# A graph-attention edge phase re-blocked: node groups at every 484th edge, four chunks to a block, TensorE work in 64-row halves

## What is computed

```python
h = (x @ W.T).reshape(n, H, D)                  # 6250 x 8 heads x 32
alpha = einsum('ehd,hd->eh', h[src], a_src) + einsum('ehd,hd->eh', h[dst], a_dst)
enc = relu(edge_attr @ edge_W.T + edge_b).reshape(-1, H, D)
alpha = leaky_relu(alpha + sum(enc * h[dst], -1), 0.2)
ex = exp(alpha - segment_max(alpha, dst)[dst])
attn = ex / maximum(segment_sum(ex, dst)[dst], 1e-10)
out = segment_sum(h[src] * attn[..., None], dst)  # sum over the edges that end in a node
```

## Time and profile before

| | |
|---|---|
| median of 3 runs | 8268.06 us (8252.19 to 8271.06) |
| the profiled execution | 8254.24 us, its span 8252.5 us |
| PE / DVE / ACT / POOL busy over the span | 75% / 56% / 35% / 52% |
| DMA engines' mean share | 31.0% of 16 engines for DMAs issued by SP, 25.4% for POOL's |
| mean granted TensorE clock | 0.923 of 2.4 GHz |

### The profile page before, as it was taken

One profiled execution on the slowest core, in us unless ns is written; L12 is line 12 of the kernel. 1 busy time (PEld: TensorE's weight loads), 2 busy tenths in 40 slices (PEclk: granted clock), 3 DMA queues, 4 the chain that ended last, 5 costly groups with the idle time before them and its releaser, 6 DMA issues. The chain is left out here.

```text
span 8252.5 us, 163611 instructions
## 1 busy us (share of the span) xinstructions
PE 6179.6 (75%) x32278; PEld 4927.6 (60%) x32278; DVE 4611.0 (56%) x15207; ACT 2868.2 (35%) x5703; POOL 4286.7 (52%) x4324
## 2 busy tenths in 40 slices
PE   0279999999999999319999176666666666663793
PEld 0166666666666666319998165555555555552792
DVE  2337777777777777611111447777777777764005
ACT  0025555555555555102222023333333333331120
POOL 0027777777777777140000437777777777771103
PEclk9989999999999999659999589999999999995896
DMA  1446666666666666625555436666666666674453
GB/s 48 144 106 155 153 153 153 153 154 155 153 153 153 153 153 154 188 87 174 186 180 184 135 91 160 159 160 160 158 157 161 159 160 159 159 147 140 162 187 129
DMA packets 1526846, 1244.98 MB, mean 151 GB/s; under 512 B 1112600, under 2 KB 1256875, under 8 KB 1500779
## 3 DMA queue, kind: packets, MB, share of 16 engines
q1 hardware_dynamic: 1316073, 648.43, 31.0%
q0 software_dynamic: 205472, 580.68, 25.4%
q10 hardware_dynamic: 5256, 15.41, 0.6%
HBM read 1106.73 MB, written 137.14 MB: 151 GB/s over the span
## 5 line engine op out<-in xcount | busy, mean ns | idle before, releaser
L732 POOL DMA_INDIRECT e_rows<-sc_table,e_idx x3900 | 3878.0, 994 | 1409.0 <-issue 1084.7
L791 PE MATMUL e_ps_o<-e_rows,e_pt 128*128 128x256 f32 x7840 | 1892.1, 389 | 475.1 <-ACT e_pt L848 455.9
L791 PEld LDWEIGHTS e_ps_o<-e_rows,e_pt 128*128 128x128 f32 x7840 | 1454.5, 194 | 735.4 <-issue 562.7
L776 PE MATMUL e_ps_s<-e_ident,e_arep 128*128 128x128 f32 x7840 | 1048.1, 282 | 344.9 <-ACT e_arep L842 341.7
L776 PEld LDWEIGHTS e_ps_s<-e_ident,e_arep 128*128 128x128 f32 x7840 | 962.1, 195 | 465.8 <-issue 460.5
L836 ACT ACTIVATE e_encr<-e_ps_e 128x640 f32<-128x640 f32 x786 | 553.5, 704 | 1353.4 <-PE e_ps_e L763 1340.0
L984 DVE CUSTOM_DVE_ANT_0 e_x<-e_ps_s,e_mask 128x640 f32<-128x640 f32 x784 | 645.1, 823 | 641.4 <-PE e_ps_s L776 631.5
L772 PE MATMUL e_ps_s<-e_encr,e_bd 128*128 128x512 f32 (+1 forms) x3136 | 956.0, 448 | 0.8 <-ACT e_encr L836 0.8
L842 ACT COPY e_arep<-e_rows 128x640 f32<-128x640 f32 x786 | 570.7, 726 | 993.9 <-DMA e_rows<-sc_table,e_idx 993.5
L1514 POOL DMA_INDIRECT c_g<-sc_yb,f_slot_i x147 | 170.9, 1162 | 1346.5 <-PEq L1496 1288.3
L772 PEld LDWEIGHTS e_ps_s<-e_encr,e_bd 128*128 128x128 f32 x3136 | 504.0, 191 | 481.9 <-issue 481.9
(11 more groups left out here) (271 smaller groups left out, 6126.7 us busy)
## 6 DMA issues: line engine op xcount, KB each, us to landing
e_dstb<-sc_dstp SPq DMA_DIRECT2D x792, 320.0 KB
x_w<-in_L_ffn_W_dram SPq DMA_DIRECT2D x112, 1024.0 KB
e_rows<-sc_table,e_idx POOLq DMA_INDIRECT x3960
x_w<-in_L_ffn_w_dram SPq DMA_DIRECT2D x60, 1024.0 KB
sc_xb<-r_zero SPq DMA_DIRECT2D x24, 1024.0 KB
x_xin<-sc_xb SPq DMA_DIRECT2D x86, 256.0 KB
sc_yb<-x_y SPq DMA_DIRECT2D x82, 256.0 KB
e_at<-sc_attrp SPq DMA_DIRECT2D x396, 45.0 KB
```

The costliest lines, as they stand in the source:

```text
L732: pool.indirect_dma_start(rows[0:CK, k, j, :], None, dr["table"][:, :], bass.IndirectOffsetOnAxis(idx[0:CK, k, j:j + 1], 0)).then_inc(s_ro ...
L776: mm = nc.tensor.matmul(banked(ps_s)[:, j, :], arep[0:CK, p, j, :, :].rearrange("p t h -> p (t h)"), ident[0:CK, 0:CK], start=not first, s ...
L791: mm = nc.tensor.matmul(ps_o[:, p, 0:D], pt[0:CK, p, j * P:(j + 1) * P], rows[0:CK, k, j, 0:D], start=(j == 0), stop=(j == CH - 1))
```

## The change

- **Windows.** A group of nodes begins at the node of every 484th edge (STEP), 427 groups; a group with more than 16 nodes is cut into windows of 16. A window still has 16 rows of nodes, but it begins at any node, and only the nodes up to the group's end count. A later group's store overwrites rows that an earlier one wrote beyond its end.
- **Blocks** have four chunks: BE = 512.
- **Row order** is head-major: partition = head x 16 + node, before node x 8 + head. `wc` and `agg` are addressed with three levels (8 heads, 16 nodes, words).
- **Score.** `bd` is 64 columns to a half; half 0 goes to PSUM rows 0 to 63, half 1 to 64 to 127, in turns by 256 edges. **Aggregation** multiplies 64 weight columns (4 heads) by the 128 columns of these heads, for each of two groups.
- **PSUM tiles** `ps_e`, `ps_s`, `ps_t` have two banks, used in turns; the encoder's 512 columns are one matmul.
- **Attributes.** `attrp` has 12 rows, and the load of a block reads them three times with a stride of zero.
- **Plan.** Group starts and ends are read with strided DMAs; the search goes over 806 pieces of 256 words and issues 14 gathers of 256 words, up to four in flight; ACT and POOL split the attributes.

```diff
-MEAN = -(-E * WIN // N)
-CH = -(-(MEAN + 2 * int(MEAN ** 0.5)) // P)
+STEP = 484
+NI = -(-E // STEP)
+MAXW = NI + -(-N // WIN)
+RB = 256
+NR = P * EC // RB
+CH = 4
...
             for s in range(2):
+                pool.wait_ge(s_rix, s + 1)
                 for t in range(WT):
                     k = s * WT + t
-                    if k:
-                        pool.wait_ge(s_cp, k)
-                    pool.indirect_dma_start(rows[:, 0, :], None, (dr["pmax"] if s == 0 else dr["smin"])[:, :],
-                                            bass.IndirectOffsetOnAxis(rix[:, s, t:t + 1], 0)).then_inc(s_wg, 16)
-                    pool.wait_ge(s_wg, 16 * (k + 1))
+                    if k >= 4:
+                        pool.wait_ge(s_cp, k - 3)
+                    pool.indirect_dma_start(found[:, k % 4, :], None,
+                                            (dr["pmax"] if s == 0 else dr["smin"]).rearrange("(r k) -> r k", k=RB),
+                                            bass.IndirectOffsetOnAxis(rix[:, s, t:t + 1], 0)).then_inc(s_wg[k % 4], 16)
...
-                sp.dma_start(wc[:, k, :], dr["wcol"].rearrange("(w t) (h c) -> w (t h) c", t=WIN, c=2)[bass.ds(w, 1), :, :]
-                             .rearrange("a p c -> (a p) c")).then_inc(s_load[k], 16)
+                sp.dma_start(wc[:, k, :], dr["wcol"][bass.ds(n, WIN), :].rearrange("t (h c) -> h t c", c=2)).then_inc(s_load[k], 16)
...
-                    sp.dma_start(at[:, k, :], dr["attrp"][:, bass.ds(e, BE)]).then_inc(s_load[k], 16)
+                    sp.dma_start(at[:, k, :], dr["attrp"][:, bass.ds(e, BE)].unsqueeze(0).to_broadcast([3, PARTS, BE])).then_inc(s_load[k], 16)
...
-                sp.dma_start(dr["agg"].rearrange("(w t) (h c) -> w (t h) c", t=WIN, c=DH)[bass.ds(w, 1), :, :]
-                             .rearrange("a p c -> (a p) c"), res[:, k, :]).then_inc(s_out, 16)
+                sp.dma_start(dr["agg"][bass.ds(n, WIN), :].rearrange("t (h c) -> h t c", c=DH), res[:, k, :]).then_inc(s_out, 16)
...
                 lhs = w_enc[:, half * P:(half + 1) * P]
-                nc.tensor.matmul(banked(ps_e)[:, 0:4, :], lhs, cols[:, 0:4, :], start=True, stop=True)
-                nc.tensor.matmul(banked(ps_e)[:, 4, :], lhs, cols[:, 4, :], start=True, stop=True).then_inc(s_enc, 1)
+                nc.tensor.matmul(ps_e[:, half, :], lhs, at[:, k, :], start=True, stop=True).then_inc(s_enc, 1)
...
-                    for half in range(2):
-                        hold(pe, s_relu, b * 2 + (half + 2), s_pp)
-                        for c0, c1 in ((0, 4), (4, CH)):
-                            nc.tensor.matmul(banked(ps_s)[:, c0:c1, :], bd[:, p, half, :], chunks(encr[:, p, half, :])[:, c0:c1, :],
-                                             start=(half == 0), stop=False, skip_group_check=True)
+                    hold(pe, s_relu, b * 2 + 3, s_pp)
+                    for c in range(0, BE, BE // 2):
+                        for half in range(2):
+                            nc.tensor.matmul(ps_s[half * (P // 2):(half + 1) * (P // 2), p, c:c + BE // 2], bd[:, p, half, :],
+                                             encr[:, p, half, c:c + BE // 2], start=(c == 0), stop=False, skip_group_check=True)
...
                 for j in range(CH):
-                    mm = nc.tensor.matmul(ps_o[:, p, 0:D], pt[0:CK, p, j * P:(j + 1) * P], rows[0:CK, k, j, 0:D],
-                                          start=(j == 0), stop=(j == CH - 1))
+                    for g in range(GROUPS):
+                        mm = nc.tensor.matmul(ps_o[g * GP:(g + 1) * GP, p, 0:GH * DH], pt[:, p, j * P + g * GP:j * P + (g + 1) * GP],
+                                              rows[:, k, j, g * GH * DH:(g + 1) * GH * DH], start=(j == 0), stop=(j == CH - 1))
```

More of the change, by code:

```diff
@@ L110, in plan_phase @@
         pt = ps("pt", [P, 512])
-        pb = ps("pb", [P, 512])
+        pb = ps("pb", [P, 1024])
         pc = ps("pc", [P, 512])
+        pn = ps("pn", [P, 2, 1024])
         s_in, s_attr, s_pad, s_const, s_pe, s_tab = (sem(n) for n in ("in", "attr", "pad", "const", "pe", "tab"))
-        s_out, s_row, s_wq, s_wg, s_bt = (sem(n) for n in ("out", "row", "wq", "wg", "bt"))
-        s_pass, s_split = sem("pass"), sem("split")
+        s_out, s_row, s_wq, s_bt, s_rix, s_zp = (sem(n) for n in ("out", "row", "wq", "bt", "rix", "zp"))
+        s_pass, s_split, s_rest, s_bl, s_grid = (sem(n) for n in ("pass", "split", "rest", "bl", "grid"))
         s_win, s_go, s_cp, s_step, s_chain, s_tile = (sem(n) for n in ("win", "go", "cp", "step", "chain", "tile"))
-        s_ends, s_scan, s_final, s_parts, s_nb, s_cum, s_blk = (sem(n) for n in ("ends", "scan", "final", "parts", "nb", "cum", "blk"))
+        s_ends, s_scan, s_final, s_iv, s_cumi, s_nb, s_cum, s_blk = (
+            sem(n) for n in ("ends", "scan", "final", "iv", "cumi", "nb", "cum", "blk"))
+        s_wg = [sem(f"wg{k}") for k in range(4)]
+        full = NI // P
         block = ctx.enter_context(nc.Block())
@@ L157, in _ @@
         def _(sp):
[L158 to L162, removed]
+            sp.wait_ge(s_pad, 1)
+            v = io["dst"]
+            sp.dma_start(dst_i[0:P - 1, :], v[0:(P - 1) * EC].rearrange("(p e) -> p e", p=P - 1)).then_inc(s_in, 16)
+            sp.dma_start(dst_i[P - 1:P, 0:E_LAST], v[(P - 1) * EC:E].rearrange("(p e) -> p e", p=1)).then_inc(s_in, 16)
+            sp.wait_ge(s_pad, 3)
             v = io["edge_attr_3"]
@@ L165, in _ @@
             sp.dma_start(attr[P - 1:P, 0:E_LAST, :], v[(P - 1) * EC:E, :].rearrange("(p e) c -> p e c", p=1)).then_inc(s_attr, 16)
-            sp.wait_ge(s_in, 64)
-            sp.wait_ge(s_pad, 6)
+            v = io["src"]
+            sp.dma_start(src_i[0:P - 1, :], v[0:(P - 1) * EC].rearrange("(p e) -> p e", p=P - 1)).then_inc(s_bl, 16)
+            sp.dma_start(src_i[P - 1:P, 0:E_LAST], v[(P - 1) * EC:E].rearrange("(p e) -> p e", p=1)).then_inc(s_bl, 16)
+            sp.wait_ge(s_final, 1)
+            sp.dma_start(dr["pmax"].rearrange("(p e) -> p e", p=P), pmax[:, :]).then_inc(s_out, 16)
+            sp.dma_start(dr["smin"].rearrange("(p e) -> p e", p=P), smin[:, :]).then_inc(s_out, 16)
+            sp.wait_ge(s_out, 32)
+            sp.wait_ge(s_zp, 2)
+            with nc.allow_non_contiguous_dma(reason="every STEP-th and every RB-th word of a sorted list, once"):
+                for s in range(2):
+                    sp.dma_start(vg[:, s, 0:full], dr["pmax"][s * STEP:s * STEP + full * P * STEP:STEP].rearrange("(t p) -> p t", p=P)).then_inc(s_grid, 16)
+                    left = dr["pmax"][(full * P + s) * STEP:E:STEP]
+                    sp.dma_start(vg[0:left.shape[0], s, full:full + 1], left.rearrange("(p e) -> p e", e=1)).then_inc(s_grid, 16)
+                for s, name in ((0, "pmax"), (1, "smin")):
+                    sp.dma_start(brow[0:1, s, :], dr[name][RB - 1:P * EC:RB].rearrange("(a r) -> a r", a=1)).then_inc(s_grid, 16)
+            sp.wait_ge(s_in, 32)
+            sp.wait_ge(s_bl, 32)
             for tile, name, r in ((dst_i, "dstp", 0), (src_i, "srcp", 1)):
@@ L228, in done, with tt, ts, whole @@
                 v.wait_ge(s_chain, steps[0])
+            def tt(o, a, b, op):
+                done(nc.vector.tensor_tensor(o, a, b, op))
+            def ts(o, a, s1, s2, *ops):
+                done(nc.vector.tensor_scalar(o, a, s1, s2, *ops))
+            def whole(o, i, m, a):
+                ts(o, i, m, a, ALU.mult, ALU.add)
+                ts(o, o, 8388608.0, None, ALU.add)
+                ts(o, o, -8388608.0, None, ALU.add)
             nc.vector.memset(dst_i[:, :], PAD_DST).then_inc(s_pad, 1)
@@ new lines, in _ @@
+            ts(vg[:, :, :], vg[:, :, :], float(N), None, ALU.min)
+            done(nc.vector.memset(vg[0:1, 0, 0:1], 0.0))
+            tt(iv[:, 0, :], vg[:, 1, :], vg[:, 0, :], ALU.subtract)
+            whole(iv[:, 1, :], iv[:, 0, :], 1.0 / WIN, 0.5 - 0.5 / WIN)
+            v.sem_inc(s_iv, 1)
+            v.wait_ge(s_pe, 4)
+            done(nc.vector.memset(offi[:, 0:1], 0.0))
+            for t in range(1, IT):
+                tt(offi[:, t:t + 1], offi[:, t - 1:t], pt[:, 7 + t:8 + t], ALU.add)
```

262 lines of the change are left out of this document (145 added, 117 removed).

## The result

The changed kernel took **9418.19 us**, median of 3 runs (9416.59 to 9427.42), against 8268.06. The ratio is 1.14 with a 95% interval of 1.137 to 1.143: 14% slower, where 1% faster was forecast. The profiled execution has a span of 9416.4 us.

What follows compares the result with a forecast made beforehand. Before, PE bounds layer 0 and POOL's gather issue layer 1; after, SP bounds layer 0. +129 (layer 0) - 181 (layer 1) - 30 (plan) = -82 on 8254.2: 8172, stated as 8175 us; 8-in-10 range 8060 to 8310.

Steps and rivals of the forecast that it cites:

- Blocks: Edge phases: 438 blocks a layer, run as 440, where the kernel before ran 392; blocks rise by 12%.
- PE per block: Layer 0: PE needs 5.72 us a block with halves in sequence, 3.84 side by side; leaned to the lower.
- Rival 2: Layer 0: PE stays the bound, halves do not overlap, width changes cost 0.17 us each; 6.9 us a block, 8305 us; 9%.
- SP becomes the bound of layer 0: Layer 0: SP's issuing of DMAs sets the pace at 6.60 us a block, 2904 us, +129 us.
- The signs I had named: Layer 0: PE under 90% busy, SP's first DMAs 6.1 to 6.4 us apart without `res` waits, POOL waiting for `htw`.
- The step that failed: SP's queue, layer 0: three-level `wc`, `at` and `agg` add at most 0.15 us a block; 0.02 was added.
- Rival 3: SP, both layers: new DMA shapes cost near 0.1 us a block, 8265 us (17%), or 0.15 or more, 8310 (4%).
- The plan's size: Plan phase before the edge phases: -30 us, between -60 and +20, from writing a third as much `attrp`.
- The number of engines: DMA engines: new `at` goes to 3, `wc` and `agg` to 8; no row prices it, sum the same.
- PE's clock: Layer 1: PE may drop oftener to 1.2 GHz; nothing in the sum, 20 us kept in the range.

Runs made afterwards that it cites:

- experiment 5: Changed kernel with `wc`, `at` and `agg` transfers flat (wrong values) and the aggregation at full width: 8102.52 us, against 8099.42 with the aggregation's halves.
- experiment 7: Changed kernel with 36 attribute rows loaded flat, the `agg` store moved to ACT's stream, and the aggregation at full width: 7849.01 us, ratio 0.951 to the kernel before.
- experiment 2: Changed kernel with 36 attribute rows written by the plan and `at` loaded as one flat transfer: 9164.39 us, 254 less than the change.
- experiment 4: Kernel before, with only the `agg` store in three levels (values land in wrong places): 8426.09 us against 8254.41.
- experiment 1: Changed kernel with `wc`, `at` and `agg` transfers all flat (wrong values), 36 attribute rows written: 8099.42 us, against 8254.41 for the kernel before.
- experiment 3: Changed kernel with `wc` read from the node table, 16 as slowest level instead of 8 (wrong values): 9376.38 us.
- experiment 6: Changed kernel with 36 attribute rows loaded flat and the `agg` store moved from SP's queue to ACT's stream: 7690.04 us, ratio 0.932 to the kernel before.

## Why the prediction was wrong

- **Blocks.** 440 a layer: the page has 880 rows of a block's DVE instruction, two layers of 440. Right.
- **PE per block.** The halves overlap, as I leaned to: 0.126 us a pass of the score and 0.064 of the aggregation, score and aggregation 1.01 and 1.03 us for 0.90 and 0.97. But the sum is 4.4 us where the lower bound was 3.84. Rival 2 was wrong on the overlap, but its price for a change of width exists, only smaller: at full clock the four stretches beside such a change take 0.06 to 0.12 us more than I had added up (`arep` 1.09 for 0.97, transposes 0.59 for 0.48), and experiments 5 and 7, which take one change away, put one at 0.10 us, where the rival had 0.17. This decides nothing here, since PE waits.
- **SP becomes the bound of layer 0.** Right, and in layer 1 too. The signs I had named are there: PE under 90%, no wait of SP for `res`, POOL waiting for `htw`.
- **The step that failed** is one sentence of the part on SP: "`wc`, `at` and `agg` become three-level, +0.15 at most ... I add 0.02". It cost 1.8 us a block in layer 0 (7.89 - 6.11) and 1.25 in layer 1 (6.13 - 4.88), for which the forecast had no term of its own at all; in layer 0 that is some ninety times the term and twelve times its upper end. I priced the new shapes by `htw`, the three-level DMA of the loop. But `htw` has the same levels on both sides (128 x 2 x 16 into 128 x 2 x 16), and the new ones have three on the DRAM side and two on the SBUF side (8 x 16 x 32 against 128 x 32). The order of the program showed this; the row that I took was near by its count of levels and far by what counts. No DMA of the loop had unequal sides, so "at most" had no ground, and the same trace had longer records on this queue in other phases: 0.56 us for `f_xs` (L1116), up to 1.09 for `x_b` (L1399). Experiments 2 (`at`) and 4 (`agg`) show the step wrong for one shape, experiment 1 for all three.
- **Rival 3** was the right mechanism with the right sign (a step of SP longer by over 0.05), but it ended at 0.15 us a block, 8310 us. With 1.8 and 1.25 its own formula, 440 x 1.8 + 440 x 1.25 = +1342 on 8175, gives 9517; the run shows 9418.
- **Without that term** the sum comes within 1%: 8099 measured for 8175, layer 0 +85 for +129, layer 1 -217 for -181, the plan -22 to -26 for -30.
- **The plan's size was luck in part.** I gave the saving to the smaller `attrp`. But experiment 1 writes all 36 rows again, and its plan ends at 310.5 us, the changed kernel's with 12 rows at 313.9 (before: 336.3). The bytes of `attrp` are not what was saved.
- **The number of engines.** "No row prices it, ... the sum is the same by either" holds for layer 0 (a turn of 49.6 us with 16 as `wc`'s slowest level, 49.4 with 8) and is 0.2 us a block off in layer 1, as far as experiment 3 shows it.
- **PE's clock.** Taken as 20 us in the range. In the changed kernel it is 0.81 of full in layer 0 and 0.66 to 0.70 in layer 1 (5800 to 8400 us, by 200 us), and PE stops for up to 4.9 us in a block. No turn shows a cost: experiments 1 and 5 have the same turns at 0.89 and 0.97.

Not settled: whether the cost comes from three levels against two, or from SBUF partitions that have to be cut into groups to match; no run here gives the SBUF side the DRAM side's levels. Nor what SP does in the 0.4 us behind such a DMA. The score's halves were never taken back, so their worth is not known; and experiments 1 to 5 are single runs.

## What to carry to other kernels

A queue that issues all loads of a loop is an engine with a budget, though it shows in no busy share: take the distance of its first DMAs from a place where it has run behind, and set every edit of a DMA against it. Change the addressing of a DMA only with the price of that very pair of shapes in hand; where a layout forces unequal sides, move the transfer to a queue that has room (experiment 6), or arrange the data once where they are written (not tried here). When an edit changes values as well as time, look whether a later phase does other work because of it: here that was 60 us of 172. And when an experiment shows a part of a change to be worth nothing (the halves, 3 us), it may only be waiting for another bound to go (159 us).

## What the hardware showed that I had not expected

- One transfer whose DRAM side is walked in three levels and whose SBUF side in two took SP 0.61 to 0.84 us to issue, where the same transfer flat took 0.33 to 0.37; after the store another 0.38 to 0.39 us passed before SP's next DMA (2.60 and 2.54 us from store to next DMA for 1.81). The size mattered little: 0.73 us for 1 KB (`wc`), 0.78 for 16 KB (`agg`), 0.81 for 36 KB (`at`), medians in layer 0 of the changed kernel.
- Two halves of 64 weight columns ran side by side with f32 data: 16 passes of 128 columns in 1.03 us, where 8 passes of 256 at full width took 1.83. Four transposes of 128 columns took 0.59 us to the start of an aggregation of 64, and 0.49 to one of 128: 0.10 us for the change.
- PE's clock in the changed kernel, late in layer 0: the same eight passes take 1.08 us in one block and 1.97 in the next, at the lower of the two levels, 1.2 GHz:

```profile
4102.85 1.08 PE L835 MATMUL e_ps_s<-e_encr,e_bd 128*64 128x256 f32 x8 [3.36 <-ACT e_encr L900]
4103.86 1.84 PE L839 MATMUL e_ps_s<-e_ident,e_arep 128*128 128x128 f32 x8
4111.78 1.97 PE L835 MATMUL e_ps_s<-e_encr,e_bd 128*64 128x256 f32 x8 [3.00 <-ACT e_encr L900]
4113.69 2.08 PE L839 MATMUL e_ps_s<-e_ident,e_arep 128*128 128x128 f32 x8
```

PE had stood for 3.36 us ahead of the fast eight and for 3.00 ahead of the slow ones, so the pause just before does not tell them apart. What the rows show is that an engine that is relieved can get slower by the instruction while the kernel does not.
